# Attention in one Trainium2 kernel: two score banks to one exponential, and the turned maxima moved to another ring of banks

## The chip, the cores and the metric

The kernel runs on one core of a Trainium2 chip. The metric is the device time of one launch in microseconds, as the median of several runs. Only the attention stage is touched; it takes about the first half of the launch.

## What is computed

The whole kernel is a layer-normed attention block, a mixture of experts, a state-space scan and the experts again, each added to the residual. The part that matters here, cut from the reference:

```python
# BATCH, N, D_MODEL, N_HEADS, RANK = 2, 2048, 256, 16, 16
Q = (x @ WQ + bQ).reshape(b, n, N_HEADS, D_K)
K = (x @ WK + bK).reshape(b, n, N_HEADS, D_K)
V = (x @ WV + bV).reshape(b, n, N_HEADS, D_K)
Qr = jnp.einsum('bnhd,dr->bnhr', Q, WQr)
Kr = jnp.einsum('bnhd,dr->bnhr', K, WKr)
scores = jnp.einsum('bnhr,bmhr->bnhm', Qr, Kr) / math.sqrt(RANK)
A = jax.nn.softmax(scores, axis=-1)
out = jnp.einsum('bnhm,bmhv->bnhv', A, V).reshape(b, n, d)
return out @ WO + bO
```

There are 32 heads (2 batches of 16), each with 2048 x 2048 scores.

## The kernel before

**Two passes over the scores.** Queries and keys are kept as bf16 parts, stacked on the partitions. A head is worked in 64 *steps*; a step is one block of 128 x 512 scores. In the *row* pass TensorE (`row_score`, L770) writes a block with queries on the partitions, and VectorE (`maxima`, L728, the reduce at L732) takes its maximum along the row. `largest` (L735) combines the 64 results of a head, GpSimd (`negate`, L652) negates them and splits them in two bf16 parts, TensorE turns them (`turn_maxima`, L828: a matmul with the identity, L830), ScalarE copies the turned maxima to SBUF (`send`, L696, L701), and SyncE's queue (`shift`, L575) writes them as two more rows of the stacked queries. In the *column* pass TensorE (`col_half`, L799, the matmul at L805, two per step) writes a block with keys on the partitions, the maximum already subtracted by those rows, ScalarE (`head`, L703, the activation at L713) takes its exponential, and TensorE (`values`, L810, the matmul at L822) multiplies the probabilities with V, into one bank `pA`. After a head's last values ScalarE copies `pA` out (`drain`, L688, L694).

**The order on TensorE is written out by hand** in `head` (L839). It goes by pairs of steps. For an even step k it issues: a row matmul for a later head, the first halves of column steps k and k+1, their second halves, and a second row matmul. The rows run LEAD = 16 steps ahead of the next head's: at column step k of head n the row steps are k+16 and k+17 of head n+1, or, from k = 48 on, k-48 and k-47 of head n+2. After every second pair (k = 2 mod 4) eight value instructions follow, for half of the preceding group of eight steps (`last_values`, L833). Below, four steps with their values are called a *round*: pair A, pair B, values. A head has 16 rounds. I number the row matmuls of a round R0 to R3 (R0 and R1 in pair A, R2 and R3 in pair B) and the reduces of the same blocks M0 to M3; R4 is the first row matmul of the next round. So in the round that begins at column step 52 the rows are steps 4 to 7 of head n+2, and R4 is that head's step 8.

**PSUM** has eight banks. Three form the row ring `pR`: a row matmul waits (`free_row`, L763) until the reduce three steps before has read the bank, so R3 waits for M0. Four form the score ring `pS`, one is `pA`. In the score ring a step's bank goes by its *place* (`place`, L546): place 57 is the bank `NT` in which the maxima are turned, just before step SIDE = 54, and three places (LEFT_OUT) hold nothing, so that 68 places fill a ring of four evenly. `free_bank` (L778) makes a column matmul wait for the exponential, or for the copy `send`, that last read its bank.

**The order on ScalarE** (`head`, L703): 64 exponentials a head, one bank each. After the first exponential of the second group (k = 8) comes `drain` of the head before; after the one of k = 55 comes `send`. The values of a head's first group (issued after column step 11) write `pA` and wait for `acc_out`, which is `drain`. VectorE's order is 48 reduces of head n+1, `largest`, 16 reduces of head n+2. All engines run heads 1 to 27 as nine turns of a loop over three heads (`heads`, L528); head 0 and heads 28 to 31 are written out.

Of the kernel before, what the change touches and what calls it, by code (L numbers as in the profile page):

```python
# [15 lines left out]
P = 128  # L16
# [8 lines left out]
KT = SEQ // P  # L25
# [433 lines left out]
def phase_attention(nc, io, x_sb, v_sb, num_dram, den_dram, inv_dram, q_dram, k_dram, sums, table):  # L459
# [10 lines left out]
    RING = 4  # L470
    SIDE = STEPS - HALF - 2
    LEFT_OUT = (16, 32, 44)
    PLACES = STEPS + 1 + len(LEFT_OUT)
    FIRST, LAST = 1, NH - 4
    assert (LAST - FIRST) % SLOTS == 0 and STEPS % SLOTS == 1 and PLACES % RING == 0
    with ExitStack() as ctx:
# [20 lines left out]
        pR = m.ps("pR", [P, 3, BANK])  # L497
# [48 lines left out]
        def place(k):  # L546

            return k + sum(k >= left for left in LEFT_OUT) + (k >= SIDE)

        SIDE_PLACE = place(SIDE) - 1  # L550
        STEP_AT = {place(k): k for k in range(STEPS)}

        def bank(at):
            return pS[:, at % RING, :]

        NT = bank(SIDE_PLACE)[0:SHIFT_ROWS * KT, 0:P]

# [128 lines left out]
        @block.scalar  # L686
        def _(act):
            def drain(n):  # L688

                act.wait_ge(summed, v(GR * n + GR))  # L690
                if not start(n):

                    act.wait_ge(acc_stored, v(16 * 2 * QC * n))
                act.activation(acc_sb[:, :], pA[:, :], ACT.Copy).then_inc(acc_out, 1)  # L694

            def send(n, s, turn_before, first=False):  # L696

                act.wait_ge(nm_turned, v(n + 1))
                if not first:
                    act.wait_ge(shift_in[(s + 2) % SLOTS], v(16 * SHIFTS * (turn_before + 1)))  # L700
                act.activation(nmT[:, :], NT, ACT.Copy).then_inc(nmT_ready, 1)  # L701

            def head(n, s, turn, ahead):  # L703
                for g in range(GR):
                    if not (start(n) and g < 2):

                        act.wait_ge(summed, v(GR * n + g - 1))
                    for j in range(HALF):
                        k = HALF * g + j
                        if j == 1 and g == 1 and not start(n):  # L710
                            drain(n - 1)
                        act.wait_ge(col_scored, v(STEPS * n + k + 1))
                        act.activation(probs[:, k % (2 * HALF), :], bank(place(k)), ACT.Exp,  # L713
                                       scale=float(DK) ** -0.5).then_inc(expd, 1)
                        if k == SIDE + 1 and ahead >= 1:
                            send(n + 1, (s + 1) % SLOTS, turn)

            load_rows(act, 0, 0, 1, True)
            load_rows(act, 0, 0, 1, False)
            send(0, 0, 0, first=True)  # L720
            heads(act, head)
            drain(NH - 1)

        @block.vector
        def _(dve):
            dve.memset(pA[:, :], 0.0).then_inc(acc_clear, 1)

            def maxima(n, s, steps):  # L728

                for k in steps:  # L730
                    dve.wait_ge(row_scored, v(STEPS * n + k + 1))
                    dve.tensor_reduce(mx4[s][:, k // QC, k % QC:k % QC + 1], pR[:, (s + k) % 3, :],  # L732
                                      AX.X, ALU.max).then_inc(maxed, 1)
# [25 lines left out]
        def _(pe):  # L759
# [3 lines left out]
            def free_row(n, s, turn, k, first=False):  # L763
                if k == 0:
                    pe.wait_ge(qk_in[s], v(16 * LOADS * (turn + 1)))
                if not first:

                    pe.wait_ge(maxed, v(STEPS * n + k - 2))

            def row_score(n, s, k):  # L770
# [4 lines left out]
                pe.matmul(pR[:, (s + k) % 3, :], q[rows, t * P:(t + 1) * P],  # L775
                          kk[rows, c * GROUP:(c + 1) * GROUP], start=True, stop=True).then_inc(row_scored, 1)

            def free_bank(n, at):  # L778

                before, n_before = at - RING, n  # L780
                if before < 0:
                    if start(n):
                        return
                    before, n_before = before + PLACES, n - 1
                if before == SIDE_PLACE:
                    if not (isinstance(n_before, int) and n_before == NH - 1):
                        pe.wait_ge(nmT_ready, v(n_before + 2))
                elif before in STEP_AT:
                    pe.wait_ge(expd, v(STEPS * n_before + STEP_AT[before] + 1))
                else:  # L790
                    free_bank(n_before, before)

            def free_col(n, s, turn, k):

                if k == 0:
                    pe.wait_ge(shift_in[s], v(16 * SHIFTS * (turn + 1)))
                free_bank(n, place(k))

            def col_half(n, s, k, half):  # L799
# [5 lines left out]
                mm = pe.matmul(bank(place(k)), kk[rows, t * P:(t + 1) * P],  # L805
# [4 lines left out]
            def values(n, s, g, half):  # L810


                if half == 0:
                    pe.wait_ge(expd, v(STEPS * n + HALF * (g + 1)))
# [13 lines left out]
            def turn_maxima(n):  # L828
                pe.wait_ge(nm_ready, v(n + 1))
                pe.matmul(NT, nm[:, :, :].rearrange("p r t -> p (r t)"), identb[:, :],  # L830
                          start=True, stop=True).then_inc(nm_turned, 1)
# [7 lines left out]
            def head(n, s, turn, ahead):  # L839
                for g in range(GR):  # L840
                    for j in range(0, HALF, 2):
                        k = HALF * g + j
                        if k == SIDE:
                            free_bank(n, SIDE_PLACE)
                            if ahead >= 1:
                                turn_maxima(n + 1)
# [24 lines left out]
            turn_maxima(0)  # L871
# [1414 lines left out]
```

## Time and profile before

| | us |
|---|---|
| median of 3 runs | 3036.11 |
| lowest and highest | 3028.75 and 3036.74 |
| profiled execution, its own time | 3029.57 |
| its span in the trace | 3027.5 |
| attention: first reduce to last drain of the sums | 141.2 to 1524.1 |

The span is the time from the first to the last recorded instruction. The profiled execution's own time is 2.07 us more. "Busy" is time in which an engine had an instruction in work. "Idle before" is idle time of that engine just before an instruction, with the engine whose event ended it. PE is TensorE, DVE is VectorE, ACT is ScalarE, POOL is GpSimd, SPq is SyncE's DMA queue. The granted clock of TensorE is given as a share of its full speed. A row of the stretches gives start and end, length, then for PE, PEld, DVE, ACT and POOL the busy us and the count, then the granted clock, the DMA share and GB/s. Instructions of one engine may overlap at their ends, so the distance from start to start is less than the duration.

### The profile page before, as it was taken

The page shows a single profiled execution, that of the slowest core. Times are in us where ns is not written, and L with a number is a line of the kernel's source. Part 1 is how long each engine was busy: PE and PEld are TensorE (multiplying, and loading weights), DVE is VectorE, ACT ScalarE, POOL GpSimd, SP SyncE. Part 2 cuts the span into 40 slices and gives each one's busy share as a digit, 9 for nine tenths or more (in the row PEclk, how much of TensorE's full clock was granted, in tenths as well). Part 3 has the DMA queues.
Part 4 walks back from the last instruction along what each step waited for, and adds up shares of the span by engine and source line. Part 5 has one row for each costly group of instructions (what it writes and reads, how often), then busy time and mean ns, then how long its engine had stood idle before and what let it go on. Part 6 is the DMA issues. An engine that isn't in the chain of part 4 may idle for free. (4 is left out here: it accounts for less than half of the span.)

```text
span 3027.5 us, 55214 instructions
## 1 busy us (share of the span) xinstructions
PE 2451.5 (81%) x14814; PEld 1114.2 (37%) x14814; DVE 2322.7 (77%) x3787; ACT 1715.4 (57%) x3510; POOL 999.1 (33%) x755
## 2 busy tenths in 40 slices
PE   7698999999999999999956977736576677597772
PEld 4322333333333323332235566612122223456662
DVE  6698999999999999999537833328799998693334
ACT  3237787878878778888815322216466565532221
POOL 3500000000000000000201566663699996146662
PEclk9879999999999999999987999967799999699997
DMA  4505111111111111111244189871343442226997
GB/s 143 133 22 166 47 35 40 47 49 47 40 35 47 49 49 40 37 45 47 91 153 132 30 217 233 204 115 19 81 115 98 117 110 66 80 77 172 228 238 202
DMA packets 255284, 294.91 MB, mean 97 GB/s; under 512 B 39121, under 2 KB 210449, under 8 KB 254929
## 3 DMA queue, kind: packets, MB, share of 16 engines
q1 hardware_dynamic: 213280, 234.30, 26.3%
q0 software_dynamic: 33104, 46.42, 8.4%
q10 hardware_dynamic: 8544, 10.11, 1.2%
q8 instruction: 143, 2.34, 0.3%
q14 instruction: 213, 1.74, 0.2%
HBM read 223.35 MB, written 66.75 MB: 96 GB/s over the span
## 5 line engine op out<-in xcount | busy, mean ns | idle before, releaser
L732 DVE TENSOR_REDUCE att_mx<-att_pR 128x1 f32<-128x512 f32 x2048 | 1266.8, 682 | 74.2 <-PE att_pR L775 73.8
L713 ACT ACTIVATE att_probs<-att_pS 128x512 f32<-128x512 f32 x2048 | 1064.3, 603 | 260.1 <-PE att_pS L805 259.6
L805 PE MATMUL att_pS<-att_q,att_k 64*128 64x512 bf16 (+1 forms) x2048 | 704.7, 381 | 0.3 <-ACT att_probs L713 0.2
L822 PE MATMUL att_pA<-att_probs,att_vh 128*17 128x512 f32 x4096 | 544.7, 604 | 8.4 <-ACT att_acc_sb L694 8.1
L775 PE MATMUL att_pR<-att_ks,att_qs 64*128 64x512 bf16 x1024 | 402.3, 393 | 48.0 <-DMA att_k<-key_parts 27.2
L775 PE MATMUL att_pR<-att_k,att_q 64*128 64x512 bf16 x1024 | 402.4, 393 | 0.7 <-DVE att_mx L732 0.7
L805 PE MATMUL att_pS<-att_qs,att_ks 64*128 64x512 bf16 (+1 forms) x2048 | 399.2, 379 | 0.2
L2161 PE MATMUL sc_pY<-sc_hc,all_ident 128*128 128x512 f32 x512 | 264.6, 642 | 124.0 <-DVE sc_hc L2118 100.0
L775 PEld LDWEIGHTS att_pR<-att_ks,att_qs 64*128 64x128 bf16 x1024 | 95.4, 93 | 561.2 <-DVE att_mx L732 490.3
L2027 POOL TENSOR_TENSOR sc_bh<-ssm_du,sc_b 128x1024 f32<-128x1024 f32 x128 | 297.5, 2357 | 9.8 <-DVE sc_hc L2118 5.6
L657 POOL TENSOR_TENSOR att_neg<-att_mx,att_minus 128x16 f32<-128x16 f32 x32 | 7.1, 221 | 853.4 <-DVE att_mx L740 853.4
L805 PEld LDWEIGHTS att_pS<-att_q,att_k 64*128 64x128 bf16 (+1 forms) x2048 | 189.9, 93 | 122.8 <-ACT att_probs L713 18.5
L2108 DVE TENSOR_TENSOR_SCAN sc_bh<-sc_pD,sc_carry,sc_bh 128x1024 f32<-128x1024 f32 x96 | 221.9, 2334 | 1.7 <-ACT sc_bh L2074 1.7
L2161 PEld LDWEIGHTS sc_pY<-sc_hc,all_ident 128*128 128x128 f32 x512 | 93.6, 199 | 275.4 <-DVE sc_hc L2118 135.8
L650 POOL COPY att_vh<-all_v 128x256 f32 (+1 forms) x32 | 12.6, 396 | 449.5 <-PE att_pA L822 449.4
L1484 DVE TENSOR_TENSOR f1e_hh<-f1e_sg,f1e_pG 64x256 f32<-64x256 f32 x64 | 27.1, 423 | 161.9 <-ACT f1e_sg L1441 161.9
L1484 DVE TENSOR_TENSOR f2e_hh<-f2e_sg,f2e_pG 64x256 f32<-64x256 f32 x64 | 27.1, 423 | 160.9 <-ACT f2e_sg L1441 160.9
L775 PEld LDWEIGHTS att_pR<-att_k,att_q 64*128 64x128 bf16 x1024 | 97.2, 95 | 115.7 <-DVE att_mx L732 115.0
L1395 POOL DMA_INDIRECT expert_sum<-f1e_y,f1e_ids x64 | 101.6, 1587 | 62.0 <-DVE f1e_y L1475 50.6
L1395 POOL DMA_INDIRECT expert_sum<-f2e_y,f2e_ids x64 | 101.6, 1587 | 60.3 <-DVE f2e_y L1475 47.7
L822 PEld LDWEIGHTS att_pA<-att_probs,att_vh 128*17 128x17 f32 x4096 | 68.3, 95 | 139.3 <-issue 69.7
L805 PEld LDWEIGHTS att_pS<-att_qs,att_ks 64*128 64x128 bf16 (+1 forms) x2048 | 103.5, 94 | 37.9 <-ACT att_probs L713 13.1
(297 smaller groups left out, 3586.9 us busy)
## 6 DMA issues: line engine op xcount, KB each, us to landing
sc_b<-scan_rows SPq DMA_DIRECT2D x128, 256.0 KB, 3.3
expert_sum<-att_zeros SPq DMA_DIRECT2D x4, 4224.0 KB, 21.6
att_qs<-query_parts SPq DMA_DIRECT2D x192, 64.0 KB, 2.1
att_q<-query_parts SPq DMA_DIRECT2D x192, 64.0 KB, 2.2
f1e_wgu<-in_w_gate SPq DMA_DIRECT2D x64, 192.0 KB, 4.1
f1e_wgu<-in_w_up SPq DMA_DIRECT2D x64, 192.0 KB, 4.1
f2e_wgu<-in_w_gate SPq DMA_DIRECT2D x64, 192.0 KB, 3.9
f2e_wgu<-in_w_up SPq DMA_DIRECT2D x64, 192.0 KB, 4.2
```

The lines of the kernel that those rows point to most:

```text
L650: pool.tensor_copy(vh[s][:, :, 0:DK], src.rearrange("p n t d -> p (n t) d")).then_inc(v_in, 1)
L657: pool.tensor_tensor(neg[:, :], mx[:, :], minus[:, :], ALU.mult).then_inc(neg_ready, 1)
L713: act.activation(probs[:, k % (2 * HALF), :], bank(place(k)), ACT.Exp, scale=float(DK) ** -0.5).then_inc(expd, 1)
L732: dve.tensor_reduce(mx4[s][:, k // QC, k % QC:k % QC + 1], pR[:, (s + k) % 3, :], AX.X, ALU.max).then_inc(maxed, 1)
L775: pe.matmul(pR[:, (s + k) % 3, :], q[rows, t * P:(t + 1) * P], kk[rows, c * GROUP:(c + 1) * GROUP], start=True, stop=True).then_inc(row_sc ...
L805: mm = pe.matmul(bank(place(k)), kk[rows, t * P:(t + 1) * P], q[rows, c * GROUP:(c + 1) * GROUP], start=not half, stop=bool(half))
L822: mm = pe.matmul(pA[32 * c:32 * c + DK + 1, :], vh[s][:, t, :], probs[:, (HALF * g + j) % (2 * HALF), :], start=(t == 0), stop=(t == KT - ...
L1395: pool.indirect_dma_start(out=sums[n % 2][:, :], out_offset=bass.IndirectOffsetOnAxis(ap=ids[:, n:n + 1], axis=0), in_=y[n % R][:, :], in_ ...
L1484: dve.tensor_tensor(hh[0:H, q, :, :].rearrange("p c n -> p (c n)"), sg[H:P, q, 0:2 * CAP], pG[H:P, q, CAP:3 * CAP], ALU.mult).then_inc(hh_ ...
L2027: pool.tensor_tensor(bh[k % H_RING][:, :, :], du[:, :, col(b, k)], b_sb[s][:, :].rearrange("p (a n) -> p a n", a=1).to_broadcast([P, DC, S ...
L2108: dve.tensor_tensor_scan(both, pD[:, k % D_RING, :, :].rearrange("p c n -> p (c n)"), both, 0.0 if k < STATES else carry[:, 0, n:n + 1], A ...
L2161: mm = pe.matmul(pY[:, c, :], ident[:, :], hc[hc_slot(k)][:, c, :], start=(n == 0), stop=(n == STATES - 1))
```

## The change

The exponentials of steps k and k+1 (k even) become one activation that reads two neighbouring banks of `pS` and writes two slots of `probs`; `expd` counts pairs. `drain` and `send` stand after a whole pair: after that of steps 8 and 9, and after that of 54 and 55. The score ring holds scores only: step k has bank k mod 4, and both column matmuls of a pair wait for the pair two before. The turned maxima go to the row ring instead: they take place 6 of the 65 places that a head now has there (NT_AT = (54+16) mod 64 = 6), between row steps 5 and 6 of head n+2. `turn_maxima` waits for the reduce of row step 3; row steps 6 and 7 wait for the reduces of steps 4 and 5 (before: 3 and 4), and row step 8 waits for the copy `send`. At the start TensorE also waits for the first `send` before head 1's rows. The diff, without the lines that only rename a bank:

```diff
@@ -467,12 +467,13 @@
     SHIFTS = 2 * SHIFT_ROWS
 
 
-    RING = 4
+    RING, ROW_RING = 4, 3
+    PAIRS = STEPS // 2
     SIDE = STEPS - HALF - 2
-    LEFT_OUT = (16, 32, 44)
-    PLACES = STEPS + 1 + len(LEFT_OUT)
+    NT_AT = (SIDE + LEAD) % STEPS
+    PLACES = STEPS + 1
     FIRST, LAST = 1, NH - 4
...
@@ -545,15 +546,14 @@
 
         def place(k):
 
-            return k + sum(k >= left for left in LEFT_OUT) + (k >= SIDE)
-
-        SIDE_PLACE = place(SIDE) - 1
-        STEP_AT = {place(k): k for k in range(STEPS)}
-
-        def bank(at):
-            return pS[:, at % RING, :]
-
-        NT = bank(SIDE_PLACE)[0:SHIFT_ROWS * KT, 0:P]
+            return k + (k >= NT_AT)
+
+        def row_bank(s, at):
+            return pR[:, (PLACES * s + at) % ROW_RING, :]
+
+        def turned_bank(s):
+
+            return row_bank((s + 1) % SLOTS, NT_AT)[0:SHIFT_ROWS * KT, 0:P]
 
...
@@ -698,21 +698,22 @@
...
-                act.activation(nmT[:, :], NT, ACT.Copy).then_inc(nmT_ready, 1)
+                act.activation(nmT[:, :], turned_bank(s), ACT.Copy).then_inc(nmT_ready, 1)
 
             def head(n, s, turn, ahead):
...
-                    for j in range(HALF):
+                    for j in range(0, HALF, 2):
                         k = HALF * g + j
-                        if j == 1 and g == 1 and not start(n):
+                        if j == 2 and g == 1 and not start(n):
                             drain(n - 1)
-                        act.wait_ge(col_scored, v(STEPS * n + k + 1))
-                        act.activation(probs[:, k % (2 * HALF), :], bank(place(k)), ACT.Exp,
+                        act.wait_ge(col_scored, v(STEPS * n + k + 2))
+                        at = k % (2 * HALF)
+                        act.activation(probs[:, at:at + 2, :], pS[:, k % RING:k % RING + 2, :], ACT.Exp,
                                        scale=float(DK) ** -0.5).then_inc(expd, 1)
-                        if k == SIDE + 1 and ahead >= 1:
+                        if k == SIDE and ahead >= 1:
                             send(n + 1, (s + 1) % SLOTS, turn)
...
@@ -729,7 +730,7 @@
...
-                    dve.tensor_reduce(mx4[s][:, k // QC, k % QC:k % QC + 1], pR[:, (s + k) % 3, :],
+                    dve.tensor_reduce(mx4[s][:, k // QC, k % QC:k % QC + 1], row_bank(s, place(k)),
                                       AX.X, ALU.max).then_inc(maxed, 1)
...
@@ -764,37 +765,29 @@
...
                 if not first:
-
-                    pe.wait_ge(maxed, v(STEPS * n + k - 2))
+                    before = place(k) - ROW_RING
+                    if before == NT_AT:
+                        pe.wait_ge(nmT_ready, v(n))
+                    else:
+
+                        last = before - (before > NT_AT) if before >= 0 else before
+                        pe.wait_ge(maxed, v(STEPS * n + last + 1))
...
-
-            def free_bank(n, at):
-
-                before, n_before = at - RING, n
-                if before < 0:
-                    if start(n):
-                        return
-                    before, n_before = before + PLACES, n - 1
-                if before == SIDE_PLACE:
-                    if not (isinstance(n_before, int) and n_before == NH - 1):
-                        pe.wait_ge(nmT_ready, v(n_before + 2))
-                elif before in STEP_AT:
-                    pe.wait_ge(expd, v(STEPS * n_before + STEP_AT[before] + 1))
-                else:
-                    free_bank(n_before, before)
 
             def free_col(n, s, turn, k):
 
                 if k == 0:
                     pe.wait_ge(shift_in[s], v(16 * SHIFTS * (turn + 1)))
-                free_bank(n, place(k))
+                if not (start(n) and k < RING):
+
+                    pe.wait_ge(expd, v(PAIRS * n + k // 2 - 1))
 
...
@@ -811,7 +804,7 @@
...
                 if half == 0:
-                    pe.wait_ge(expd, v(STEPS * n + HALF * (g + 1)))
+                    pe.wait_ge(expd, v(PAIRS * n + HALF // 2 * (g + 1)))
...
                     mm.then_inc(summed, 1)
 
-            def turn_maxima(n):
+            def turn_maxima(n, s, ahead):
                 pe.wait_ge(nm_ready, v(n + 1))
-                pe.matmul(NT, nm[:, :, :].rearrange("p r t -> p (r t)"), identb[:, :],
+                if ahead >= 1 and not start(n):
+                    pe.wait_ge(maxed, v(STEPS * (n + 1) + NT_AT - ROW_RING + 1))
+                pe.matmul(turned_bank(s), nm[:, :, :].rearrange("p r t -> p (r t)"), identb[:, :],
                           start=True, stop=True).then_inc(nm_turned, 1)
...
@@ -841,9 +836,8 @@
                     for j in range(0, HALF, 2):
                         k = HALF * g + j
                         if k == SIDE:
-                            free_bank(n, SIDE_PLACE)
                             if ahead >= 1:
-                                turn_maxima(n + 1)
+                                turn_maxima(n + 1, (s + 1) % SLOTS, ahead - 1)
...
@@ -868,7 +862,8 @@
             for k in range(STEPS):
                 free_row(0, 0, 0, k, first=(k < 3))
                 row_score(0, 0, k)
-            turn_maxima(0)
+            turn_maxima(0, 0, NH - 1)
+            pe.wait_ge(nmT_ready, 1)
```

## Rows read from the trace of the kernel before

**Rows 1.** The page: TensorE's granted clock in tenths, over 40 slices.

```profile
PEclk9879999999999999999987999967799999699997
```

**Rows 2.** Stretches: one head inside the loop, 40.50 us long.

```profile
1138.00:1178.50 40.50, 40.27 (x323) 12.78 (x321) 39.74 (x66) 33.77 (x67) 1.01 (x4) 1.00 0.16 45
```

**Rows 3.** The page's costliest groups (busy us, mean ns, idle before).

```profile
L732 DVE TENSOR_REDUCE att_mx<-att_pR 128x1 f32<-128x512 f32 x2048 | 1266.8, 682 | 74.2 <-PE att_pR L775 73.8
L713 ACT ACTIVATE att_probs<-att_pS 128x512 f32<-128x512 f32 x2048 | 1064.3, 603 | 260.1 <-PE att_pS L805 259.6
```

**Rows 4.** Timeline of one ordinary round (start us, us, what, [idle before]).

```profile
804.41 0.39 PE L775 MATMUL att_pR<-att_ks,att_qs 64*128 64x512 bf16 x1
...
804.86 0.38 PE L805 MATMUL att_pS<-att_q,att_k 34*128 34x512 bf16 x1
...
805.06 2.06 ACT L713 ACTIVATE att_probs<-att_pS 128x512 f32<-128x512 f32 x4 [0.41 <-PE att_pS L805]
...
805.59 0.39 PE L775 MATMUL att_pR<-att_k,att_q 64*128 64x512 bf16 x1
...
805.90 1.05 PE L822 MATMUL att_pA<-att_probs,att_vh 128*17 128x512 f32 x8
...
806.89 0.39 PE L775 MATMUL att_pR<-att_ks,att_qs 64*128 64x512 bf16 x1
```

**Rows 5.** Timeline of VectorE before the first head's scores.

```profile
182.73 7.85 DVE L732 TENSOR_REDUCE att_mx<-att_pR 128x1 f32<-128x512 f32 x13
```

**Rows 6.** Timeline of VectorE over one head.

```profile
812.54 4.95 DVE L732 TENSOR_REDUCE att_mx<-att_pR 128x1 f32<-128x512 f32 x8
817.82 12.38 DVE L732 TENSOR_REDUCE att_mx<-att_pR 128x1 f32<-128x512 f32 x20 [0.34 <-PE att_pR L775]
830.49 22.28 DVE L732 TENSOR_REDUCE att_mx<-att_pR 128x1 f32<-128x512 f32 x36 [0.29 <-PE att_pR L775]
852.90 0.22 DVE L740 TENSOR_REDUCE att_mx<-att_mx 128x16 f32<-128x64 f32 x1
```

**Rows 7.** Timeline of the round in which ScalarE drains the sums.

```profile
827.29 0.39 PE L775 MATMUL att_pR<-att_ks,att_qs 64*128 64x512 bf16 x1
...
827.94 0.60 ACT L713 ACTIVATE att_probs<-att_pS 128x512 f32<-128x512 f32 x1 [0.41 <-PE att_pS L805]
...
828.44 0.59 ACT L694 ACTIVATE att_acc_sb<-att_pA 128x512 f32<-128x512 f32 x1
...
829.08 1.05 PE L822 MATMUL att_pA<-att_probs,att_vh 128*17 128x512 f32 x8 [0.23 <-ACT att_acc_sb L694]
```

**Rows 8.** Timeline of the round that turns the maxima.

```profile
814.57 0.39 PE L775 MATMUL att_pR<-att_ks,att_qs 64*128 64x512 bf16 x1
...
815.33 0.23 PE L830 MATMUL att_pS<-att_identb,att_nm 128*32 128x128 bf16 x1
...
817.28 0.26 ACT L701 ACTIVATE att_nmT<-att_pS 32x128 bf16<-32x128 f32 x1
...
817.40 0.39 PE L775 MATMUL att_pR<-att_ks,att_qs 64*128 64x512 bf16 x1
```

**Rows 9.** One line's ScalarE copies out of two banks (ns min/median/max).

```profile
L1089 ACT ACTIVATE f_xnT_all<-f1r_pT x8: 1001/1008/1019, 1589.7 to 1630.7; 128x1024 f32<-128x1024 f32 x8
```

**Rows 10.** Timeline of VectorE at one of the loop's jumps.

```profile
866.15 0.69 DVE L732 TENSOR_REDUCE att_mx<-att_pR 128x1 f32<-128x512 f32 x1 [2.86 <-PE att_pR L775]
...
870.38 4.96 DVE L732 TENSOR_REDUCE att_mx<-att_pR 128x1 f32<-128x512 f32 x8 [1.42 <-PE att_pR L775]
...
898.04 0.22 DVE L740 TENSOR_REDUCE att_mx<-att_mx 128x16 f32<-128x64 f32 x1
```

**Rows 11.** Stretch right after that jump (columns as in rows 2).

```profile
866.00:870.00 4.00, 4.00 (x22) 1.20 (x23) 2.66 (x4) 2.17 (x4) 0.00 (x0) 0.57 0.35 97
```

**Rows 12.** Timeline of TensorE in the last head.

```profile
1491.47 1.05 PE L822 MATMUL att_pA<-att_probs,att_vh 128*17 128x512 f32 x8 [0.82 <-ACT att_acc_sb L694]
```

**Rows 13.** Timeline of ScalarE in the last head.

```profile
1493.10 10.63 ACT L713 ACTIVATE att_probs<-att_pS 128x512 f32<-128x512 f32 x20 [0.30 <-PE att_pS L805]
```

More of the change, by code:

```diff
@@ L467, in phase_attention @@
     SHIFTS = 2 * SHIFT_ROWS
-    RING = 4
+    RING, ROW_RING = 4, 3
+    PAIRS = STEPS // 2
     SIDE = STEPS - HALF - 2
-    LEFT_OUT = (16, 32, 44)
-    PLACES = STEPS + 1 + len(LEFT_OUT)
+    NT_AT = (SIDE + LEAD) % STEPS
+    PLACES = STEPS + 1
     FIRST, LAST = 1, NH - 4
-    assert (LAST - FIRST) % SLOTS == 0 and STEPS % SLOTS == 1 and PLACES % RING == 0
+    assert (LAST - FIRST) % SLOTS == 0 and SLOTS == ROW_RING and STEPS % RING == 0 and SIDE % 2 == 0
     with ExitStack() as ctx:
@@ L495, in phase_attention @@
         inv = m.sb("inv", [P, INV])
-        pR = m.ps("pR", [P, 3, BANK])
+        pR = m.ps("pR", [P, ROW_RING, BANK])
         pS = m.ps("pS", [P, RING, BANK])
@@ L774, in row_score @@
                 t, c = k // QC, k % QC
-                pe.matmul(pR[:, (s + k) % 3, :], q[rows, t * P:(t + 1) * P],
+                pe.matmul(row_bank(s, place(k)), q[rows, t * P:(t + 1) * P],
                           kk[rows, c * GROUP:(c + 1) * GROUP], start=True, stop=True).then_inc(row_scored, 1)
-            def free_bank(n, at):
-                before, n_before = at - RING, n
-                if before < 0:
-                    if start(n):
-                        return
-                    before, n_before = before + PLACES, n - 1
-                if before == SIDE_PLACE:
-                    if not (isinstance(n_before, int) and n_before == NH - 1):
-                        pe.wait_ge(nmT_ready, v(n_before + 2))
-                elif before in STEP_AT:
-                    pe.wait_ge(expd, v(STEPS * n_before + STEP_AT[before] + 1))
-                else:
-                    free_bank(n_before, before)
             def free_col(n, s, turn, k):
@@ L804, in col_half @@
                 rows = slice(at, at + (MAX_ROWS, REST_ROWS)[half])
-                mm = pe.matmul(bank(place(k)), kk[rows, t * P:(t + 1) * P],
+                mm = pe.matmul(pS[:, k % RING, :], kk[rows, t * P:(t + 1) * P],
                                q[rows, c * GROUP:(c + 1) * GROUP], start=not half, stop=bool(half))
```

## The prediction

> **What bounds the kernel now.** I read the page first. TensorE's clock is near full through the attention stage, slices 4 to 20 [rows 1]; the two largest groups are the reduces, with little idle time before them, and the exponentials, with much [rows 3]. The stretch of one head says the same more sharply: of 40.50 us TensorE is busy 40.27, VectorE 39.74, ScalarE 33.77 [rows 2]. So ScalarE, whose work the change shortens, has 6.7 us to spare in every head, and a gain can only come through what TensorE or VectorE waits for.
>
> Which of the two sets the pace? VectorE alone is not full: before the first head's column scores, 13 reduces take 7.85 us, and with 0.68 for the last that is (7.85 - 0.68) / 12 = 0.598 us from start to start [rows 5]. Four would take 2.39 us. A round takes 806.89 - 804.41 = 2.48 us (finer reading of many rounds: 2.474) [rows 4]. The pace is a loop through both engines: R0 of a round starts, M0 can start 0.42 later (817.40 to 817.82) [rows 6, 8], R3 waits for M0 to read the bank and starts 1.18 after R0 (804.41 to 805.59), the values 0.31 after R3, and R4 0.99 after the values [rows 4]: 1.18 + 0.31 + 0.99 = 2.48. **Whatever delays the values or R4 in a round therefore delays everything, in full**, as VectorE has only 2.474 - 2.392 = 0.08 us of room per round.
>
> The head's period confirms this. VectorE's own order shows two idle stretches in a head, 0.34 and 0.29 us [rows 6]. The first ends at row step 8, in the round of column step 52 that turns the maxima: R4 comes 817.40 - 814.57 = 2.83 after R0, 0.35 late [rows 8]. The second is in the round of step 8: the values start 829.08 - 827.29 = 1.79 after R0 and not 1.49, held by `drain`, 0.30 late [rows 4, 7]. Then 16 x 2.474 + 0.35 + 0.30 = 40.23, and `largest`, which waits for the last reduce to be written, adds the other 0.27 of 40.50. No third stall is left for the three empty places of the score ring: filling them is worth nothing while rows are being made. Each of the nine jumps of the loop costs more, 898.04 - 852.90 = 45.14 for that head, 4.64 extra, with TensorE's instructions late and no engine named [rows 6, 10].
>
> **The change, part by part.** *The paired exponential.* The trace has none. Four single ones take 2.06 us, 0.60 the last, so (2.06 - 0.60) / 3 = 0.487 from start to start, 0.11 less than their duration [rows 4, 7]. A two-bank copy out of PSUM takes 1.008 us, 1.001 to 1.019 [rows 9]. Single and copy have the same fixed part as far as rows show, so I take 1.02 - 0.11 = 0.91 from the start of a pair to the start of what follows; bounds are 0.89 (the fastest copy, same overlap) and 0.974 (two singles, nothing saved). The saving is 0.06 us a pair, 2 us a head, all on ScalarE and hidden in its 6.7 us idle. In an ordinary round the pair A starts when step k+1 is written: its second half starts 0.45 after R0 (804.86) plus 0.42, so 0.87; single ones start at 0.65 (805.06). Pair B then runs from 1.78 to 2.80. The columns that reuse its banks come in the next pair B, 2.474 + 0.67 = 3.14: 0.29 of slack with 0.05 for the signal. Steady rounds: zero.
>
> The Trainium skill ("ScalarE: Activation LUTs", What ACT_TABLE_LOAD costs) gives 186 ns + 0.833 ns per element without pointer operands, and an overlap of 93 ns. By that a pair occupies the engine for an estimated 0.946 us, against 0.519 for a single; the first is a little over my 0.91, the second over the row's 0.487. The sum below would be 2 us higher by it.
>
> *`drain` behind a whole pair.* It could start at 1.15 (828.44), after one exponential [rows 7]. Now it stands behind the pair of steps 8 and 9: 0.87 + 0.91 = 1.78, plus 0.59 of its own and 0.05 for the signal (829.03 to 829.08) gives values at 2.42 where 1.79 was. **+0.63 us**, nothing covers it: ScalarE's order is first in, first out, and behind the values stands R4, and behind R4 VectorE. This is late in heads 1 to 30, 30 times (head 31 has no rows; see the tail).
>
> *The turned maxima in the row ring.* In the round of step 52 R0, R1 and the turning matmul stay at 0, 0.45 and 0.76 (815.33) [rows 8]; its wait for row step 3's reduce ends about 0.55. The stall on the score bank in pair B goes. But row step 6 (R2) now needs M0, as R3 does in an ordinary round: 1.18 [rows 4], where a plain order would have it at about 0.92. R3 needs M1, 0.60 later: 1.78. Values at 2.09, R4 by this path at 3.08. R4 also waits for `send`, and this is later: the second column of pair B has its second half at 1.18 + 0.43 = 1.61, its pair of exponentials starts at 2.03, `send` at 2.94, and it ends 0.26 later [rows 8], so R4 is at 3.25. Before it was 2.83. **+0.42 us**, in heads 0 to 29, 30 times. Between bounds: 0.25 if `send` were in time, 0.49 with a pair of 0.974. Nothing absorbs it: VectorE would start M4 at 2.81 and gets it at 3.67.
>
> Behind `send` stand SyncE's four transfers for the next head. They start 0.05 before R4 now where they started 0.15 after it, and the next head's first column is two rounds after R4 in both: more room than before, cost nothing. SyncE's and GpSimd's queues are not reordered. TensorE's waits are as many as before or fewer.
>
> *Start and tail.* The wait for the first `send` holds head 1's rows for one copy, 0.4 us once. In the last head there are no rows; 20 exponentials take 10.63 us, so a round of 2.13 is ScalarE's pace [rows 13], and TensorE alone needs nearly as much. Pairs give back 0 to 2 us over 20 rounds; the drain there held the values 0.82 us already [rows 12] and holds them some 0.3 longer. I take -1.
>
> **Sum:** 30 x (0.63 + 0.42) + 0.4 - 1 = +31 us. The profiled execution would go from 3029.6 to 3061; it is 6.5 below the median of the runs shown, 3036.1, so the median goes to **3067**, 1.0% slower. Within 0.3%, 9 us, a measurement of this kernel can't tell from no change (the three runs of before span 8 us).
>
> **Rivals.** *A: only one of the two stalls grows.* `send` may be covered (then the side stall costs 0.25, sum 26), or a wait is not as I order it and a whole term is missing: +12 without the drain's 19, +18 without the side's 13. Medians 3048 to 3062. For it: the score ring's own stall goes. Against: both waits are first in, first out, with their price in rows. 0.13.
>
> *B: the new gaps lower TensorE's clock.* At a jump VectorE waits 2.86 us for TensorE, and in the 4 us after it TensorE's granted clock is 0.57, near the lower level of 1.2 GHz [rows 10, 11]; that is most of what the 4.64 us hold beyond the 2.86: 1.8 us. Each of the 60 stalls could do that: up to +108, 3175; in a quarter of them +27, 3094. Against it: in the last head TensorE waited 0.82 us for `drain`, and the eight value instructions after it take 1.05 us as in an ordinary round at full clock [rows 4, 12]; the largest new gap is 0.93. 0.05.
>
> *C: faster, by the jumps.* ScalarE's loop of three heads loses 96 activations and their waits. If the jumps stall because all engines fetch instructions at once, the nine stalls of 4.64 us, 42 us, could shrink; from three quarters of them gone (31 of 42) the change wins, and with all gone it ends at 3025. For it: no engine is named as the releaser there. Against: the engine that is late is TensorE, whose instructions stay the same. 0.04. The Trainium skill ("Runtime: NRT & Kernel Launch", Instruction fetch mechanics) says that a taken branch outside the window held forces a fetch of the target before the engine goes on. By that rule TensorE's stall stays, and the trace, which shows TensorE late at every jump, agrees.
>
> *D: the paired read is slow or split* (two banks read as two instructions, the change not doing what it says). Then 0.974 to 1.2 per pair: both stalls grow by 0.06 to 0.29, +4 to +17, 3071 to 3084. 0.06. ScalarE becomes the bound of a round only from 1.237 a pair on.
>
> *E: nearly no change*, the stalls hidden by room that I misread, within 9 us: 0.06.
>
> My own case has 0.66. Its range takes the bounds above (-5 for the send path, +5 for 0.974) and the spread of the runs: 3053 to 3078. The range to hold 8 in 10 reaches into A and D: 3046 to 3086. Faster is C and 0.01 of E, 0.05. Within 0.3% are the other 0.05 of E and 0.02 at the low end of A, 0.07. Slower is the rest, 0.88.
>
> **What would show it.** In the profile after: 1024 exponentials of 128x1024 with a mean near 1.02 us, ScalarE busy less by some 60 us. VectorE's two idle stretches a head near 0.93 (released by the round whose values wait for `att_acc_sb`) and 0.77 (at row step 8), their sum 1.05 over before; a head's period of 41.55 us. Idle before `send`'s reader R4, released by ScalarE's `send`. A round elsewhere still 2.474. The prediction is wrong if rounds elsewhere change, if the drain round's values start by 1.8 after R0, if R4 of the turning round comes before 3.0, if the granted clock falls at these gaps, or if the jumps cost other than 4.6 us.

## The result

| | before | after |
|---|---|---|
| median | 3036.43 us (4 runs) | 3062.26 us (4 runs, 3057.86 to 3062.45) |
| ratio | 1 | 1.0088, 95% interval 1.0068 to 1.0108 |
| profiled execution, own time | 3029.57 | 3062.24 |
| its span | 3027.5 | 3060.5 |
| usual period of a head | 40.50 | 41.57 |

The change costs 26 us in the medians and 33 us in the profiled executions; forecast were 31 us and 3067. It is slower, and each of the two stalls is as large as forecast.

The page of the kernel after: engine totals, the granted clock, and the two groups that answer to [rows 3].

```profile
PE 2450.7 (80%) x14814; PEld 1117.6 (37%) x14814; DVE 2324.9 (76%) x3787; ACT 1651.9 (54%) x2486; POOL 1000.0 (33%) x755
...
PEclk9879999999999999999986999967799999698996
...
L733 DVE TENSOR_REDUCE att_mx<-att_pR 128x1 f32<-128x512 f32 x2048 | 1267.7, 684 | 108.8 <-PE att_pR L781 108.4
L714 ACT ACTIVATE att_probs<-att_pS 128x1024 f32<-128x1024 f32 x1024 | 999.7, 1022 | 358.5 <-PE att_pS L798 356.2
```

The paired exponential takes 1.022 us, 1024 of them, and ScalarE is busy 999.7 us with them instead of 1064.3. It got nothing for it: its idle time rose from 260 to 358 us. The reduces are as they were, but VectorE idled 108.8 us before them and not 74.2. That is where the time went. Over one head, from one combining of the maxima (L741) to the next, as in [rows 6]:

```profile
830.22 0.22 DVE L741 TENSOR_REDUCE att_mx<-att_mx 128x16 f32<-128x64 f32 x1
830.36 4.95 DVE L733 TENSOR_REDUCE att_mx<-att_pR 128x1 f32<-128x512 f32 x8
836.08 12.38 DVE L733 TENSOR_REDUCE att_mx<-att_pR 128x1 f32<-128x512 f32 x20 [0.77 <-PE att_pR L781]
849.38 22.28 DVE L733 TENSOR_REDUCE att_mx<-att_pR 128x1 f32<-128x512 f32 x36 [0.92 <-PE att_pR L781]
871.79 0.22 DVE L741 TENSOR_REDUCE att_mx<-att_mx 128x16 f32<-128x64 f32 x1
```

The same two idle stretches stand after the same reduces, 0.77 and 0.92 us instead of 0.34 and 0.29. The busy stretches between them have not changed by 0.01 us: 4.95, 12.38, 22.28. The period is 871.79 - 830.22 = 41.57.

The timeline of the drain's round, all engines, to be read against [rows 7]:

```profile
803.98 0.39 PE L781 MATMUL att_pR<-att_ks,att_qs 64*128 64x512 bf16 x1
...
804.42 0.38 PE L798 MATMUL att_pS<-att_q,att_k 34*128 34x512 bf16 x1
...
804.83 1.02 ACT L714 ACTIVATE att_probs<-att_pS 128x1024 f32<-128x1024 f32 x1 [0.54 <-PE att_pS L798]
...
805.75 0.59 ACT L694 ACTIVATE att_acc_sb<-att_pA 128x512 f32<-128x512 f32 x1
...
806.40 1.05 PE L815 MATMUL att_pA<-att_probs,att_vh 128*17 128x512 f32 x8 [0.86 <-ACT att_acc_sb L694]
...
807.38 0.39 PE L781 MATMUL att_pR<-att_ks,att_qs 64*128 64x512 bf16 x1
```

The pair starts 0.85 after R0 (forecast 0.87), the drain 0.92 after the pair (0.91), and the values 2.42 after R0 (2.42). Step 9's second column half, at 804.42, is what the pair waits for. In the round that turns the maxima, against [rows 8]:

```profile
790.83 0.39 PE L781 MATMUL att_pR<-att_ks,att_qs 64*128 64x512 bf16 x1
...
791.58 0.23 PE L825 MATMUL att_pR<-att_identb,att_nm 128*32 128x128 bf16 x1
...
792.00 0.39 PE L781 MATMUL att_pR<-att_ks,att_qs 64*128 64x512 bf16 x1 [0.19 <-DVE att_mx L733]
...
792.60 0.39 PE L781 MATMUL att_pR<-att_k,att_q 64*128 64x512 bf16 x1
...
793.77 0.25 ACT L701 ACTIVATE att_nmT<-att_pR 32x128 bf16<-32x128 f32 x1
...
794.08 0.39 PE L781 MATMUL att_pR<-att_ks,att_qs 64*128 64x512 bf16 x1
```

R2 waits for M0 and comes 1.17 after R0 (forecast 1.18), R3 at 1.77 (1.78), the copy `send` starts at 2.94 (2.94), and R4 comes at 3.25 (3.25), 0.06 after the copy's end. R4 was at 2.83. As forecast, it is the copy that releases R4: of the waits that `send`'s copy ends, 31, one a head, are those of a row matmul's weight load, 32.7 us in all.

### The profile page after: what moved, and what is told of

Its sections match the earlier page's. It is cut to its first block and busy times, and to the rows that moved or that the text cites. A ratio compares the mean times of both kernels' runs of the same rounds, so it can differ in the third digit from the quotient of the medians.

```text
span 3060.5 us, 53324 instructions
## 1 busy us (share of the span) xinstructions
PE 2450.7 (80%) x14814; PEld 1117.6 (37%) x14814; DVE 2324.9 (76%) x3787; ACT 1651.9 (54%) x2486; POOL 1000.0 (33%) x755
## 5 line engine op out<-in xcount | busy, mean ns | idle before, releaser
L733 DVE TENSOR_REDUCE att_mx<-att_pR 128x1 f32<-128x512 f32 x2048 | 1267.7, 684 | 108.8 <-PE att_pR L781 108.4
L714 ACT ACTIVATE att_probs<-att_pS 128x1024 f32<-128x1024 f32 x1024 | 999.7, 1022 | 358.5 <-PE att_pS L798 356.2
L798 PE MATMUL att_pS<-att_qs,att_ks 64*128 64x512 bf16 (+1 forms) x2048 | 407.8, 380 | 0.0
```

What stands on the lines that cost most here:

```text
L714: act.activation(probs[:, at:at + 2, :], pS[:, k % RING:k % RING + 2, :], ACT.Exp, scale=float(DK) ** -0.5).then_inc(expd, 1)
L733: dve.tensor_reduce(mx4[s][:, k // QC, k % QC:k % QC + 1], row_bank(s, place(k)), AX.X, ALU.max).then_inc(maxed, 1)
L798: mm = pe.matmul(pS[:, k % RING, :], kk[rows, t * P:(t + 1) * P], q[rows, c * GROUP:(c + 1) * GROUP], start=not half, stop=bool(half))
```

## The experiments

The whole launch can hide a few microseconds, as the loop's jumps cost different amounts from one jump to the next and from one kernel's trace to another's. So each run is read by its ratio and by the usual distance between two combinings of the maxima in the loop, the period of a head. The ratios are against the kernel before, on the same chip. The last column has the launch as it was forecast and as its median came out, on chips where the kernel before took 3033 to 3036 us.

| run | ratio, 95% interval | period forecast | period measured | launch forecast, measured |
|---|---|---|---|---|
| kernel before | 1 | | 40.50 | 3036 |
| kernel after | 1.0088, 1.0068 to 1.0108 | 41.55 | 41.57 | 3067, 3062 |
| drain first | 1.0021, 1.0006 to 1.0036 | 40.65 | 40.64 to 40.77 | 3034, 3040 |
| singles | 1.0106, 1.0083 to 1.0129 | 41.27 | 41.34 | 3053, 3068 |
| send first | 1.0091, 1.0068 to 1.0114 | 41.40 | 41.38 | 3057, 3064 |
| drain first, kernel before | 0.9975, 0.9955 to 0.9996 | 40.21 | 40.21 | 3027, 3030 |
| turned at the start | 1.0038, 1.0022 to 1.0053 | 41.05 | 40.83 | 16 below the kernel after, 3045 |
| both repairs | 0.9928, 0.9903 to 0.9954 | 40.10 | 39.90 | 3024, 3014 |
| and one reduce first | 0.9944, 0.9925 to 0.9963 | 39.89 | 39.70 | 3018, 3016 |
| the same with singles | 0.9929, 0.9909 to 0.9950 | 39.89 | 39.70 | none, 3012 |
| drain late | 1.0340, 1.0315 to 1.0365 | 42.50 | 44.03 | 3090, 3138 |
| both repairs, kernel before | 0.9932, 0.9911 to 0.9953 | 39.9 | 39.90 | 3018, 3016 |

**Drain first.** One part of the change undone, and more: the drain goes ahead of the pair.

```diff
-                        if j == 2 and g == 1 and not start(n):
+                        if j == 0 and g == 1 and not start(n):
                             drain(n - 1)
```

> The changed kernel with the drain of the sums ahead of the exponentials of steps 8 and 9 instead of behind them. My theory: the 0.92 us that VectorE idles per head in that round is only the drain standing behind a pair (0.87 + 0.91 + 0.59 + 0.05 = 2.42). Ahead of the pair ScalarE is free from 0.33 us after the round's start, so the drain ends near 0.9 and holds nothing: the idle stretch goes to 0, a head's period from 41.57 to 40.65 us, 30 times 0.92 = 28 us less, about 3034. Rival, that the pair itself or the ring of two pairs holds the values in that round: the period stays at 41.57, or falls only to the 0.29 us of before (40.94, 3043).

VectorE's timeline of one head:

```profile
396.46 0.22 DVE L741 TENSOR_REDUCE att_mx<-att_mx 128x16 f32<-128x64 f32 x1
396.60 4.94 DVE L733 TENSOR_REDUCE att_mx<-att_pR 128x1 f32<-128x512 f32 x8
402.31 34.66 DVE L733 TENSOR_REDUCE att_mx<-att_pR 128x1 f32<-128x512 f32 x56 [0.77 <-PE att_pR L781]
437.10 0.22 DVE L741 TENSOR_REDUCE att_mx<-att_mx 128x16 f32<-128x64 f32 x1
```

The stretch of 0.92 is gone, 56 reduces run on, and the other stands untouched at 0.77. The period is 40.64 here and up to 40.77 in other heads; what those have more was not looked into. So the drain's place is the whole of this stall. The launch took 3040 against a forecast of 3034.

**Singles.** The pairing undone, its positions kept.

```diff
-                        act.wait_ge(col_scored, v(STEPS * n + k + 2))
-                        act.activation(probs[:, at:at + 2, :], pS[:, k % RING:k % RING + 2, :], ACT.Exp,
-                                       scale=float(DK) ** -0.5).then_inc(expd, 1)
+                        for half in range(2):
+                            act.wait_ge(col_scored, v(STEPS * n + k + half + 1))
+                            one = act.activation(probs[:, at + half, :], pS[:, k % RING + half, :], ACT.Exp,
+                                                 scale=float(DK) ** -0.5)
+                        one.then_inc(expd, 1)
```

> The changed kernel with each paired exponential split in two of one bank, everything else kept (counting by pairs, drain and send behind the pair, turned maxima in the row ring). It splits the 31 us into what comes from the positions and what from the pairing itself. My theory: the first exponential can start 0.22 us sooner and two take 0.97 against 0.92, so the drain comes 0.15 sooner (idle 0.77 instead of 0.92), and R4 of the turning round comes at 3.10 instead of 3.25 (idle 0.62 instead of 0.77): period 41.27, 9 us less, about 3053. Rival one, the pairing is all of it: period near 40.5 again, about 3030. Rival two, the positions are all of it: 41.57, 3062.

```profile
437.88 0.22 DVE L743 TENSOR_REDUCE att_mx<-att_mx 128x16 f32<-128x64 f32 x1
438.02 4.95 DVE L735 TENSOR_REDUCE att_mx<-att_pR 128x1 f32<-128x512 f32 x8
443.66 12.38 DVE L735 TENSOR_REDUCE att_mx<-att_pR 128x1 f32<-128x512 f32 x20 [0.69 <-PE att_pR L783]
456.82 22.27 DVE L735 TENSOR_REDUCE att_mx<-att_pR 128x1 f32<-128x512 f32 x36 [0.78 <-PE att_pR L783]
479.22 0.22 DVE L743 TENSOR_REDUCE att_mx<-att_mx 128x16 f32<-128x64 f32 x1
...
524.89 0.22 DVE L743 TENSOR_REDUCE att_mx<-att_mx 128x16 f32<-128x64 f32 x1
```

Forecast were idle stretches of 0.62 and 0.77; these are 0.69 and 0.78. Of the 1.07 us a head that the change costs, pairing by itself is 41.57 - 41.34 = 0.23, and the places of drain, copy and turned maxima are the other 0.84. The launch did not follow: 3068 where I wrote 3053. The heads are shorter by 30 x 0.23 = 7 us than in the kernel after, and the jumps took it back. A jump's extra is the distance across it less the period, 524.89 - 479.22 - 41.34 = 4.33 here; the loop's eight sum to 40.6 us, against 33.1 in the kernel after. More on this below.

**Send first.** The copy goes ahead of the exponentials of steps 54 and 55.

```diff
+                        if k == SIDE and ahead >= 1:
+                            send(n + 1, (s + 1) % SLOTS, turn)
                         act.wait_ge(col_scored, v(STEPS * n + k + 2))
                         ...
-                        if k == SIDE and ahead >= 1:
-                            send(n + 1, (s + 1) % SLOTS, turn)
```

> The changed kernel with the copy of the turned maxima (send) ahead of the exponentials of steps 54 and 55. The copy is then done 2.1 us after R0, so R4 is no longer held by it. My theory has a second limit right behind: the turned bank takes one of the three row banks, so R2 and R3 wait for M0 and M1, and R4 comes at 3.08 instead of 3.25: idle 0.60 instead of 0.77, period 41.40, 5 us less, about 3057. Rival, that only send holds R4 and the lost row bank costs nothing: R4 at 2.73 (a plain round plus the turning matmul's 0.25), idle near 0.25, period 41.05, 16 us less, about 3046.

```profile
437.87 0.22 DVE L741 TENSOR_REDUCE att_mx<-att_mx 128x16 f32<-128x64 f32 x1
438.00 4.95 DVE L733 TENSOR_REDUCE att_mx<-att_pR 128x1 f32<-128x512 f32 x8
443.54 12.38 DVE L733 TENSOR_REDUCE att_mx<-att_pR 128x1 f32<-128x512 f32 x20 [0.59 <-PE att_pR L781]
456.84 22.28 DVE L733 TENSOR_REDUCE att_mx<-att_pR 128x1 f32<-128x512 f32 x36 [0.92 <-PE att_pR L781]
479.25 0.22 DVE L741 TENSOR_REDUCE att_mx<-att_mx 128x16 f32<-128x64 f32 x1
```

0.59 against 0.60 forecast, and 0.25 by the rival. Two limits lay one behind the other. With the copy out of the way the lost row bank still holds R4: R3 can't be sooner than M1 allows. The launch missed its forecast here too, 3064 instead of 3057: the jumps, which sum to 43.3 us, took back more than the 6 us of the shorter heads.

**Drain first, kernel before.** The kernel before had the same fault in small.

```diff
-                        if j == 1 and g == 1 and not start(n):
+                        if j == 0 and g == 1 and not start(n):
                             drain(n - 1)
```

> The kernel before, with the drain ahead of the exponential of step 8. My theory: its idle stretch of 0.29 us in that round goes to 0, the period from 40.50 to 40.21, 9 us less, about 3027. Rival, that the stretch comes from the left-out place 16 of the score ring: no change.

The period is 40.21, as forecast; the left-out place 16 costs nothing. The ratio, 0.9975, fits 9 us.

**Turned at the start.** The remedy for the second stall: turn the maxima where no reduce and no matmul soon after needs that bank. The diff is against the kernel after, and has the two moved lines of `send` as well.

```diff
-    SIDE = STEPS - HALF - 2
+    SIDE = STEPS - HALF - 4
```

> The changed kernel with the maxima turned two steps earlier, at the start of the round of step 52 (right behind the values, before R0), and the copy send ahead of that step's exponentials; the drain stays behind its pair. The turned bank then takes the place before row step 4, so the row matmul that waits for the copy is R2, which comes 0.9 us later anyway, and no reduce is needed sooner. My theory: only the turning matmul's own time on TensorE is left, 0.25 us, so that idle stretch goes from 0.77 to 0.25 and the period from 41.57 to 41.05 us, 16 us less without the loop's jumps. Rival, that giving up one of three row banks costs by itself wherever it is done: idle stays at 0.5 to 0.6, period 41.3 to 41.4.

```profile
394.11 17.35 DVE L733 TENSOR_REDUCE att_mx<-att_pR 128x1 f32<-128x512 f32 x28
412.39 22.28 DVE L733 TENSOR_REDUCE att_mx<-att_pR 128x1 f32<-128x512 f32 x36 [0.92 <-PE att_pR L781]
```

The stretch of 0.77 is gone altogether, so giving up a row bank costs nothing in this place, against the rival. The period is 40.83 and not 41.05: the turning costs next to nothing. The next run shows where the price went.

**Both repairs.** This, and the drain first.

> The same with the drain ahead of the exponentials of steps 8 and 9 as well: both stalls that the change enlarged are removed, its paired exponentials and its row ring are kept. My theory: period 16 x 2.474 + 0.27 + 0.25 = 40.10 us, against 40.50 before the change and 41.57 after it, so 12 us under the kernel before (about 3024) if the loop's jumps cost what they did there. Rival, that the pairs hold something in other rounds once these stalls are gone: period 40.5 or more.

Its timeline from the values to the first row matmul of the round of step 52, and VectorE over the head:

```profile
437.19 1.05 PE L815 MATMUL att_pA<-att_probs,att_vh 128*17 128x512 f32 x8
438.06 0.22 PE L825 MATMUL att_pR<-att_identb,att_nm 128*32 128x128 bf16 x1
438.21 0.39 PE L781 MATMUL att_pR<-att_ks,att_qs 64*128 64x512 bf16 x1
...
438.40 0.27 ACT L701 ACTIVATE att_nmT<-att_pR 32x128 bf16<-32x128 f32 x1 [0.17 <-PE att_pR L825]
```

```profile
436.00 0.22 DVE L741 TENSOR_REDUCE att_mx<-att_mx 128x16 f32<-128x64 f32 x1
436.13 39.63 DVE L733 TENSOR_REDUCE att_mx<-att_pR 128x1 f32<-128x512 f32 x64
475.89 0.22 DVE L741 TENSOR_REDUCE att_mx<-att_mx 128x16 f32<-128x64 f32 x1
```

R0 comes 438.21 - 437.19 = 1.02 after the values, 0.03 more than the 0.99 of an ordinary round. Behind the values the turning matmul costs 0.03 us; between two pairs of 64-row matmuls it had cost 0.25 (R2 in the kernel before came at 0.92 and not at 0.67). My 0.25 was a row read in another place. The matmul uses all 128 rows, as the values do; that this is why it is cheap behind them was not tested. All 64 reduces now form one stretch, and the kernel is faster than both: 39.90 us a head.

**And one reduce first.** `largest` after the next head's first reduce.

```diff
                     maxima(n + 1, s1, range(LEAD, STEPS))
+                if ahead >= 2:
+                    maxima(n + 2, s2, range(1))
+                if ahead >= 1:
                     largest(n + 1, s1)
                 if ahead >= 2:
-                    maxima(n + 2, s2, range(LEAD))
+                    maxima(n + 2, s2, range(1, LEAD))
```

> The same, and VectorE takes the next head's first reduce before it combines a head's 64 maxima. The 0.21 us for which that instruction waits for the last reduce then lie under a reduce; its own 0.14 remains against VectorE's room of 0.08 per round. My theory: 0.27 becomes 0.06, period 39.89 us, 6 us less than the run before, about 3018. Rival, that GpSimd's three instructions are now late for the turning matmul (they end 0.3 us before it by my count): the gain is given back there, 40.1 or more.

Periods of 39.68 to 39.71, 0.2 less than the run before, as forecast. They are 0.19 below the forecast period for the same reason as in the run before: the turning matmul costs 0.22 less than I took. The ratios of the two runs overlap, so the time of the whole launch doesn't show the extra step.

**The same with singles.**

> The same once more, with each paired exponential split in two of one bank. What is the pairing itself worth? My theory: nothing, as ScalarE is never waited for: ScalarE busier by some 2 us a head, the same period of 39.89 within 0.05. Rival, that the pair's shorter time or its fewer PSUM reads beside VectorE's help: 0.1 us or more a head longer.

ScalarE's costliest group in this run and in the one before it:

```profile
L717 ACT ACTIVATE att_probs<-att_pS 128x512 f32<-128x512 f32 x2048 | 1057.2, 604 | 238.1 <-PE att_pS L803 238.0
```

```profile
L716 ACT ACTIVATE att_probs<-att_pS 128x1024 f32<-128x1024 f32 x1024 | 993.1, 1021 | 303.5 <-PE att_pS L801 303.4
```

64 us more of busy time, 65 us less of idle time, the same period. Where nothing waits for ScalarE, the pairing is worth nothing.

**Drain late.** The suspected cost a second time.

```diff
-                        if j == 2 and g == 1 and not start(n):
+                        if j == 4 and g == 1 and not start(n):
                             drain(n - 1)
```

> The changed kernel with the drain one pair later still, behind the exponentials of steps 10 and 11: the suspected cost once more. My theory: it starts at 0.87 + 2 x 0.92 = 2.71 us after R0, the values at 3.35 instead of 2.42, and all of it reaches the end: idle 0.92 becomes 1.85, period 42.50 instead of 41.57, 28 us more, about 3090. Rival one, that part of a longer stall is absorbed by the queues: less than 0.8 a head. Rival two, that a gap of 1.85 us in TensorE's work lowers its granted clock, which 0.92 did not: clearly more than 0.93 a head, with matmuls of 0.6 us and more behind the gap.

Two of its heads on VectorE, the second one the usual case, and the drain's round in that second one:

```profile
520.66 22.28 DVE L733 TENSOR_REDUCE att_mx<-att_pR 128x1 f32<-128x512 f32 x36 [1.84 <-PE att_pR L781]
...
563.76 0.69 DVE L733 TENSOR_REDUCE att_mx<-att_pR 128x1 f32<-128x512 f32 x1 [2.45 <-PE att_pR L781]
564.65 1.95 DVE L733 TENSOR_REDUCE att_mx<-att_pR 128x1 f32<-128x512 f32 x3 [0.20 <-PE att_pR L781]
567.17 19.81 DVE L733 TENSOR_REDUCE att_mx<-att_pR 128x1 f32<-128x512 f32 x32 [0.58 <-PE att_pR L781]
```

```profile
561.74 1.45 PE L815 MATMUL att_pA<-att_probs,att_vh 128*17 128x512 f32 x8 [1.78 <-ACT att_acc_sb L694]
563.12 0.60 PE L781 MATMUL att_pR<-att_ks,att_qs 64*128 64x512 bf16 x1
...
566.75 0.39 PE L781 MATMUL att_pR<-att_ks,att_qs 64*128 64x512 bf16 x1
```

Where the clock holds, the stall is 1.84, as forecast, and passes through in full: the head from 220.25 to 262.74 is 42.49 long (forecast 42.50). But in 24 of the 30 heads rival two is right. TensorE stood 1.78 us, the eight value instructions behind it took 1.45 us instead of 1.05, and the row matmuls 0.60 instead of 0.39 until 566.75. The granted clock from 562.5 to 565.5 is 0.50, the lower of the two levels, 1.2 instead of 2.4 GHz. That is 2.45 + 0.20 + 0.58 = 3.23 us of idle in place of 1.85, and a period of 44.03. So 0.92 us of standing still cost 0.92, and 1.85 us cost about 3.4. This is my rival B, which the change itself escaped: behind every one of TensorE's 31 waits for `drain` in the kernel after, 0.86 us in most heads, the granted clock is 1.00.

**Both repairs, kernel before.**

```diff
-    SIDE = STEPS - HALF - 2
+    SIDE = STEPS - HALF - 4
 ...
-                        if j == 1 and g == 1 and not start(n):
+                        if j == 0 and g == 1 and not start(n):
                             drain(n - 1)
+                        if k == SIDE and ahead >= 1:
+                            send(n + 1, (s + 1) % SLOTS, turn)
                         act.wait_ge(col_scored, v(STEPS * n + k + 1))
 ...
-                        if k == SIDE + 1 and ahead >= 1:
-                            send(n + 1, (s + 1) % SLOTS, turn)
```

> The kernel before, with single exponentials and the turned maxima still in the score ring, but with the two repairs: the drain ahead of the exponential of step 8, the maxima turned at the start of the round of step 52 and the copy send ahead of that step's exponential. My theory: the same 39.9 us a head as the repaired changed kernel, so that neither the pairs nor the row ring has a part in what the best version gains; about 3018. Rival, that the score ring with its left-out places holds TensorE once the rest is gone: 40.1 or more.

39.90 us a head, as with pairs and row ring. So neither part of the change has a share in the gain; the gain is the two positions.

## Why the prediction was right

*What sets the pace.* The loop of 2.474 us through R0, M0, R3 and the values stood: where nothing interrupts them, 64 reduces take 39.63 us, (39.63 - 0.68) / 63 x 4 = 2.473 for four. That a delay of the values or of R4 passes in full was the step on which all else hangs, and it was tested three ways: taken away in the kernel after (0.92 gone, period 0.80 to 0.93 less), taken away in the kernel before (0.29 gone, 0.29 less), and doubled (1.84 where the clock held).

*The drain behind a pair*, forecast +0.63, measured 0.92 - 0.29 = 0.63.

*The turned maxima in the row ring*, forecast +0.42, measured 0.77 - 0.34 = 0.43. Both halves of the step were right: the copy is the last limit (send first took 0.18 off), the lost row bank the one behind it.

*The pair's duration*, 1.02 with 0.91 to what follows, is 1.022 and 0.92. ScalarE's saving is 1715.4 - 1651.9 = 63.5 us, forecast some 60. The estimate of 0.946 us by the Trainium skill ("ScalarE: Activation LUTs", What ACT_TABLE_LOAD costs) is 0.03 more than the 0.92 measured.

*Start and tail.* Head 1's first row matmul comes 0.48 us later (180.88 to 181.36; forecast 0.4). From the last combining of the maxima to the last drain it is 1557.7 - 1512.1 = 45.6 us instead of 1523.5 - 1476.5 = 47.0, so -1.4 (forecast -1).

*The sum.* In the trace the combinings of the first and the last head lie 1332.6 us apart instead of 1297.0, 35.6 more. 30 heads by 1.07 are 32; the loop's eight jumps back took 33.1 instead of 31.2 us over the period, and one long wait for a DMA before them 9.5 instead of 9.3, 2 more together; the rest is the start and heads that run 0.1 long. With the tail's -1.4, and 1 us less behind the attention, the span grew by 33.0.

*The term that was mis-sized* is in none of the prediction's sums but in those of the runs that followed: the turning matmul's own 0.25 us. It is 0.03 behind the values. *The jumps* are what the prediction read wrong. It took one of them, 4.64 us, for all, and counted nine. But a loop of nine turns jumps back eight times, and in the kernel before the eight cost 2.5 to 4.7 us, 31.2 in all and not 37. The ninth long wait, 9.3 us over the period, is none of the loop's: in the kernel before TensorE stands 7.53 us before a row matmul at 268.25 us until the DMA `att_k<-key_parts` has landed. The prediction named jumps of another cost than 4.6 as a sign of being wrong, and the sign came; the forecast was spared by a bit of luck, as their sums before and after differ by only 2 us, while in singles and send first they differ by 9 and 12. The median lay some 7 us above the profiled execution before, and level with it after, so the jumps may also be the 5 us between 3067 and 3062; that is argued, not shown.

Of the rivals, A (one stall covered), D (a slow pair) and E are excluded by the rows above. B is real for longer waits: the clock fell behind none of TensorE's waits of 0.86 us, and behind most of those of 1.78 us. C, that fewer ScalarE instructions would shrink the jumps, finds no support: 33.1 us after against 31.2 before.

## What to carry to other kernels

Merging instructions on an engine with slack gained nothing here, and it made every short instruction queued behind the merged one wait for the whole of it. The merging itself cost 0.23 us a head; that the drain, the copy and the turned maxima changed their places cost 0.84. Before merging, list what stands between them or right behind (here a drain and a copy that TensorE waits for) and put it ahead. When an item is moved into another ring, count what it takes from that ring just then: one of three banks moved every wait up by one reduce; in a place where the next users came late it cost nothing. Find the loop that sets the pace by adding start-to-start distances until they close (1.18 + 0.31 + 0.99 = 2.48); a stall on it could then be forecast to a few hundredths here.

## What the runs showed that I had not expected

The turning matmul, over all 128 rows, costs 0.03 us behind the values, which are over 128 rows too, and 0.25 us between matmuls of 64 rows each, although its own duration is 0.22 or 0.23 in both.

The extra of a jump of the loop, over the head's period, runs from 2.4 to 5.9 us. In the kernel after, one of the short ones is 915.81 - 871.79 - 41.57 = 2.45:

```profile
871.79 0.22 DVE L741 TENSOR_REDUCE att_mx<-att_mx 128x16 f32<-128x64 f32 x1
...
884.90 7.56 DVE L733 TENSOR_REDUCE att_mx<-att_pR 128x1 f32<-128x512 f32 x12 [2.29 <-PE att_pR L781]
...
915.81 0.22 DVE L741 TENSOR_REDUCE att_mx<-att_mx 128x16 f32<-128x64 f32 x1
```

What a jump costs goes by the clock. Three jumps, each from 2 us before TensorE's first matmul behind the wait to 8 us after it, in the columns of [rows 2]; the first two are of the kernel after, the third of singles:

```profile
882.48:892.48 10.00, 7.14 (x60) 2.66 (x60) 7.63 (x13) 5.96 (x8) 0.40 (x1) 1.00 0.41 98
497.47:507.47 10.00, 8.00 (x52) 2.50 (x52) 6.07 (x10) 4.40 (x5) 0.40 (x1) 0.83 0.38 102
877.57:887.57 10.00, 8.01 (x41) 2.50 (x42) 5.11 (x8) 4.34 (x8) 0.00 (x0) 0.66 0.36 98
```

In the first the granted clock stayed at 1.00, and only the wait was paid, 2.45 us. In the second it averaged 0.83, and the price was 4.61; in the third it averaged 0.66, twice the loss, and the price was 5.53. The traces of all kernels but drain late hold 88 such jumps, and each falls in one of these three groups: 6 at 1.00 cost 2.4 to 2.8 us, 47 at 0.83 cost 4.0 to 4.9, and 35 at 0.66 cost 5.3 to 5.9. So about 3 us of the dearest jumps are the clock's, and singles and send first, whose jumps sum to 40.6 and 43.3 us, have six and seven of the third group where the kernel after has one. The Trainium skill ("Runtime: NRT & Kernel Launch", Instruction fetch mechanics) explains a gap at a taken branch, where its target is outside the window held, by the fetch of the target. The traces agree in that TensorE stands at all eight jumps for 2.2 to 3.0 us without a releaser; they do not show the fetch itself. What decides between the three groups stays open. It is not the length of TensorE's wait alone: a wait of 2.23 us kept the clock at one jump and is in the group of 0.66 at another, and of the waits of 1.78 us in drain late 5 kept it.
